# An audio tower on one core: streams laid out time by time, layer 4 in three blocks, and each quad of samples turned alone

## What is computed

```python
h = x[:, None, :]                                    # (64, 1, 4000)
for w, g, b, s in zip(conv_ws, ln_gs, ln_bs, strides):   # 7 convolutions over time, 128 channels
    h = conv1d(h, w, s)                              # taps 10,3,3,3,3,2,2; strides 5,2,2,2,2,2,2
    h = gelu(layernorm_over_channels(h) * g + b)
h = layernorm(h, fln_g, fln_b) @ proj_w + proj_b     # (64, 12, 192)
h = h + attention(layernorm(h))                      # 6 heads over the 12 tokens of a clip
h = h + ffn(layernorm(h))                            # 9 experts: expert 0 for all, the best one for each token
```

## Time and profile before

| | |
|---|---|
| median of 3 runs | 563.9 us (563.47 to 564.89) |
| the profiled execution's own time | 564.41 us |
| its span | 562.6 us |
| TensorE matmul busy | 537.1 us, 95% |
| ScalarE, VectorE, GpSimd busy | 322.7, 309.5, 258.6 us |
| mean granted TensorE clock | 0.98 |

### The profile page before, as it was taken

One profiled execution on the slowest core, in us unless ns is written; L12 is line 12 of the kernel. 1 busy time (PEld: TensorE's weight loads), 2 busy tenths in 40 slices (PEclk: granted clock), 3 DMA queues, 4 the chain that ended last, 5 costly groups with the idle time before them and its releaser, 6 DMA issues.

```text
span 562.6 us, 11208 instructions
## 1 busy us (share of the span) xinstructions
PE 537.1 (95%) x4099; PEld 504.7 (90%) x4099; DVE 309.5 (55%) x767; ACT 322.7 (57%) x557; POOL 258.6 (46%) x298
## 2 busy tenths in 40 slices
PE   6898999999999999999999999999999997899995
PEld 6797989999999999999999999999899886799995
DVE  4665465457567666757575766654564443612231
ACT  1567657747675776677575757773663423444440
POOL 5683464785239427732863394243242120033343
PEclk9999999999999999999999999999999996799998
DMA  7490001692000100000000000000000087151110
GB/s 196 124 276 10 1 15 35 171 239 59 20 1 20 24 5 7 20 22 5 2 20 20 7 20 1 20 6 2 2 6 6 0 218 193 40 142 44 45 39 12
DMA packets 19505, 29.46 MB, mean 52 GB/s; under 512 B 2620, under 2 KB 13846, under 8 KB 19452
## 3 DMA queue, kind: packets, MB, share of 16 engines
q1 hardware_dynamic: 16140, 18.95, 12.7%
q0 software_dynamic: 3296, 9.78, 6.9%
q10 hardware_dynamic: 16, 0.00, 0.0%
HBM read 17.09 MB, written 9.18 MB: 47 GB/s over the span
## 4 chain that ended last, share of the span: by engine, by line
PE 88%; ACT 3%; POOL 2%; DVE 2%; issue 2%; DMA 0%; SPq 0%; POOLq 0%; DVEq 0%; ACTq 0%
PE ps L805 23%; PE ps L797 11%; PE ps L794 8%; PE ps L824 7%; PE ps L1076 5%; PE ps L878 4%; PE ps L1065 3%; PE ps L1064 3%; PE ps L899 3%; PE ps L799 2%; PE ps L795 2%; PE ps L944 2%; PE ps L967 2%; PE ps L887 2%; PE ps L888 1%
## 5 line engine op out<-in xcount | busy, mean ns | idle before, releaser
L649 POOL TENSOR_TENSOR rstd<-ssum,neghalf 128x4 f32<-128x4 f32 (+8 forms) x128 | 116.3, 908 | 195.8 <-DVE ssum L1180 195.4
L805 PE MATMUL ps<-wt,wide 128*124 128x128 f32 (+3 forms) x1248 | 149.5, 274 | 2.5 <-ACT wide L1517 2.1
L805 PEld LDWEIGHTS ps<-wt,wide 128*124 128x124 f32 (+3 forms) x1248 | 142.7, 180 | 5.5 <-issue 2.8
L1486 ACT ACTIVATE work<-ps 128x512 f32<-128x512 f32 (+8 forms) x128 | 66.3, 518 | 131.9 <-PE ps L805 73.0
L1189 DVE TENSOR_TENSOR work<-ps,rstd 128x512 f32<-128x512 f32 (+8 forms) x128 | 75.3, 588 | 75.4 <-POOL rstd L649 71.6
L1180 DVE TENSOR_REDUCE ssum<-work 128x4 f32<-128x516 f32 (+8 forms) x128 | 74.8, 584 | 57.3 <-ACT work L1486 56.9
L643 POOL TENSOR_TENSOR rstd<-var,half 128x12 f32<-128x12 f32 (+3 forms) x39 | 79.0, 2039 | 7.8 <-DVE var L1117 7.2
L1528 ACT ACTIVATE h<-ps,lncol 128x512 f32<-128x512 f32 (+1 forms) x120 | 79.7, 712 | 1.8 <-PE ps L878 1.8
L1503 ACT ACTIVATE wide<-ps,lncol 128x256 f32<-128x256 f32 (+1 forms) x112 | 74.1, 770 | 2.2 <-PE ps L824 2.1
L797 PE MATMUL ps<-wt,h 128*128 128x256 f32 x288 | 70.1, 380 | 0.0
L824 PE MATMUL ps<-ident,work 128*128 128x128 f32 (+3 forms) x416 | 64.8, 268 | 1.2 <-ACT wide L1503 0.8
(11 more groups left out here) (239 smaller groups left out, 825.5 us busy)
## 6 DMA issues: line engine op xcount, KB each, us to landing
sorted_tokens<-zero POOLq DMA_DIRECT2D x1, 5886.5 KB, 30.4
W2s<-in_L_ffn_W_dram SPq DMA_DIRECT2D x9, 576.0 KB, 8.4
wide<-in_L_ffn_W_dram SPq DMA_DIRECT2D x8, 576.0 KB
cols<-cols SPq DMA_DIRECT2D x24, 128.0 KB, 2.2
cols<-sorted_tokens SPq DMA_DIRECT2D x13, 96.5 KB, 1.9
xnat<-in_x_dram SPq DMA_DIRECT2D x7, 130.0 KB, 2.1
wt<-in_L_ffn_b_dram SPq DMA_DIRECT2D x1, 864.0 KB, 5.0
wide<-in_L_tok_conv_w_dram SPq DMA_DIRECT2D x4, 192.0 KB, 3.1
```

The lines of the kernel that those rows point to most:

```text
L649: gp.tensor_tensor(rstd[0:rows, idx, 0:count], ssum[0:rows, idx, 0:count], neghalf[0:rows, 0:count], ALU.pow).then_inc(rstd_done, 1)
L805: last = nc.tensor.matmul(y[0:rows, j * C:(j + 1) * C], h[l - 1][g % 2][:, at:at + rows], wt[:, TAP0[l] + tap, :], start=(tap == 0), stop= ...
L1486: nc.scalar.activation(sq[0:rows, n % 2, 0:CUTS[l][k], 0:C], ybank(n)[0:rows, 0:w].rearrange("p (j c) -> p j c", c=C), ACT.Square).then_in ...
```

## The change

**Layout.** Rows and streams now lie time by time: time 0 of the eight clips, time 1 of the eight clips, and so on. The rows of a sample tile are 16 segments x 8 clips. An odd or even stream is a run of 8 clips per time. There are no unused rows between clips, so the blocks are of 120, 112, 128, 96 and 96 rows in layers 2 to 6 (124, 116, 100, 100, 104 before), and layer 4 takes three blocks a group where it took four. The cuts of layer 2 are 4, 4, 2, 3 (4, 3, 3, 3 before). The paddings go, and with them most of the memsets that cleared them.

**Quads.** `is_pair`, `halves` and `other_copies` go. `xhl` holds a local step's taps as high, low, high, low (40 columns), so a triple is 120 columns, and `xt` turns 17 triples in every group. VectorE copies a quad once, as 120 rows. `xcol` has two buffers (three before). The 24 DMAs that copied halves and the waits on them go.

**Other.** The first weights `w0t` are built on 120 partitions with a simpler mask; `projg` and `w0per` have tiles of their own. `HEAD`, `BODY`, `LAST`, `DRAIN` and the `RUN_` tables are written anew.

```diff
-ROWS_OF = [P, P, 124, 116, 100, 100, 104]
+ROWS_OF = [P, P, 120, 112, P, 96, 96]
-CUTS = [None, (4, 4, 4, 4, 4, 4, 1), (4, 3, 3, 3), (4, 3), (4,), (2,), (1,)]
+CUTS = [None, (4, 4, 4, 4, 4, 4, 1), (4, 4, 2, 3), (4, 3), (3,), (2,), (1,)]
 BODY = [
     ((1, 0, 0), [('xt', 0, 2)], []),
-    ((1, 0, 1), [], []),
+    ((1, 0, 1), [('l0', 0, 2, 0), ('l0', 0, 2, 2)], []),
     ((4, -2, 0), [('l0', 0, 2, 1)], []),
-    ((2, -1, 1), [('l0', 0, 2, 0)], []),
-    ((2, -1, 0), [('l0', 0, 2, 2)], []),
-    ((2, -1, 2), [('l0', 0, 3, 0), ('raw', 1)], []),
-    ((5, -2, 0), [('l0', 0, 3, 2), ('l0', 0, 3, 1)], []),
+    ((2, -1, 2), [], []),
+    ((2, -1, 1), [('raw', 1), ('xt', 0, 3)], []),
+    ((2, -1, 0), [('l0', 0, 3, 1)], []),
+    ((5, -2, 0), [('l0', 0, 3, 0), ('l0', 0, 3, 2)], []),
...
-    ((1, 0, 3), [('xt', 1, 0)], []),
-    ((3, -1, 0), [], [('xs', 1, 1)]),
-    ((3, -1, 1), [('l0', 1, 0, 1), ('l0', 1, 0, 0)], []),
-    ((1, 0, 5), [('l0', 1, 0, 2), ('l0', 1, 1, 1)], []),
-    ((1, 0, 6), [('l0', 1, 1, 0), ('l0', 1, 1, 2)], []),
+    ((1, 0, 3), [('l0', 0, 4, 2), ('xt', 1, 0)], [('pow', 1, 3), ('pow', 1, 4)]),
+    ((3, -1, 0), [('l0', 1, 0, 1), ('l0', 1, 0, 0)], [('pow', 1, 2)]),
+    ((1, 0, 5), [('l0', 1, 0, 2), ('xt', 1, 1)], []),
+    ((3, -1, 1), [('l0', 1, 1, 1), ('l0', 1, 1, 2)], [('xs', 1, 1)]),
+    ((1, 0, 6), [('l0', 1, 1, 0)], []),
 ]
...
 (scale, on VectorE)
-                parts = halves(g, lo, hi)
-                for src, dst in parts:
-                    last = nc.vector.tensor_copy(dst[:, :, :, 0:ROW].bitcast(F32R), src)
-                last.then_inc(s_high, 1)
+                twice = xsc[:, lo:hi, :].unsqueeze(2).to_broadcast([P, n, 2, K0])
+                nc.vector.tensor_copy(xhl5[:, lo:hi, :, 0, :].bitcast(F32R), twice).then_inc(s_high, 1)
                 ve.wait_ge(s_high, k)
-                for src, dst in parts:
-                    last = nc.vector.tensor_tensor(dst[:, :, :, ROW:2 * ROW].bitcast(F32R), src, dst[:, :, :, 0:ROW], ALU.subtract)
-                last.then_inc(s_parts, 1)
+                nc.vector.tensor_tensor(xhl5[:, lo:hi, :, 1, :].bitcast(F32R), twice, xhl5[:, lo:hi, :, 0, :],
+                                        ALU.subtract).then_inc(s_parts, 1)
...
 (job_xt, on VectorE)
-                if is_pair(g, q):
-                    nc.vector.tensor_copy(xcol[m % XC][0:64, 0:w], src[0:64, 0:w]).then_inc(s_upper, 1)
-                    nc.vector.tensor_copy(xcol[last % XC][64:P, 0:w], src[64:P, 0:w]).then_inc(j_dve, 1)
+                nc.vector.tensor_copy(xcol[(QUADS * g + q) % 2][0:12 * K0, 0:w], src[0:12 * K0, 0:w]).then_inc(j_dve, 1)
...
 (SyncE)
-                sp.wait_ge(s_upper, 2 * (g - PAIRED_FROM) + q // 2 + 1)
-                sp.dma_start(up[64:P, :], up[0:64, :]).then_inc(s_dup[m % XC], 16)
-                sp.wait_ge(j_dve, DVE_TO[JOB[("xt", g, q)] + 1])
-                sp.dma_start(low[0:64, :], low[64:P, :]).then_inc(s_dup[(m + 1) % XC], 16)
...
 (turn of layer 1, on TensorE: where a block's rows go in PSUM)
-                        to = bass.AP(at.tensor, at.offset, [at.ap[0], [1, P // 2], [P if d else 3 * P, 2]])
+                        to = bass.AP(at.tensor, at.offset, [at.ap[0], [2 * BT, SEG // 2], [P if d else 3 * P, 2], [1, BT]])
...
 (gelu of layer 1, on ScalarE)
-                        to = bass.AP(at.tensor, at.offset, [at.ap[0], [shift, v.stop - v.start], [1, w], [LEN1, P // 2]])
+                        to = bass.AP(at.tensor, at.offset, [at.ap[0], [BT * shift, v.stop - v.start], [BT * LEN1, SEG // 2], [1, w * BT]])
...
 (gelu of layer 6)
-                    dst = h6[:, :].rearrange("p (b t) -> p b t", b=BT)
+                    dst = h6[:, :].rearrange("p (b t) -> p t b", b=BT)
...
-RUN_7 = {'turn_h': 3, 'stat_h': 2, 'power_h': 2, 'project': 3, ...
+RUN_7 = {'turn_h': 2, 'stat_h': 2, 'power_h': 2, 'project': 4, ...
 (DRAIN, behind the chunk (6, 7, 0))
     (None, [('down', 3)], []),
+    (None, [('up', 2, 1)], []),
+    (None, [('up', 2, 0)], []),
+    (None, [('up', 2, 3), ('up', 2, 2)], []),
+    (None, [('down', 4)], []),
     (None, [], []),
-    (None, [('up', 2, 1), ('up', 2, 0)], []),
-    (None, [('up', 2, 2), ('down', 4), ('up', 2, 3)], []),
     (None, [], []),
     (None, [('up', 2, 5)], []),
```

More of the change, by code:

```diff
@@ L74, in needed @@
     ends = [ROWS_OF[layer - 1] * sum(CUTS[layer - 1][:i + 1]) for i in range(len(CUTS[layer - 1]))]
-    return next((i for i, e in enumerate(ends) if e > 2 * rows), len(ends) - 1)
+    return next((i for i, e in enumerate(ends) if e >= 2 * rows + BT), len(ends) - 1)
 def first_block(layer, k):
@@ L266 @@
             assert ORDER.index((1, was_[0], reads_)) <= min(slot_of(("l0", g_, q_, j)) for j in range(3))
-        if g_ >= 1 and q_ < 2:
-            part_ = next(k for k, row in enumerate(SLOTS) if ("xs", g_, q_) in row[2])
-            assert slot_of(("xt", g_ - 1, (1 if g_ < PAIRED_FROM else 0, 2 if g_ == PAIRED_FROM else 4)[q_])) <= part_
-STEPS = [[] for _ in SLOTS]
-RUN_0 = {'turn_h': 3, 'stat_h': 3, 'power_h': 4, 'project': 5, 'stat_1': 5, 'power_1': 4, 'norm_1': 6, 'turn_1': 8, 'copy_1': 7, 'qkv': 9, 'split_queries': 9, 'split_keys': 9, 'scores': 10, 'mask': 10, 'less_max': 10, 'exp': 10, 'sum_probs': 10, 'turn_probs': 11, 'copy_probs': 11, 'values': 12, 'divide': 12, 'turn_heads': 14, 'copy_heads': 14, 'out_project': 15, 'residual': 15, 'power_2': 15, 'norm_2': 16, 'turn_2': 17, 'copy_2': 17, 'logits': 18, 'choose': 18, 'rank': 21, 'slot': 21, 'scatter': 27, 'fold_weights': 0, 'fold': 1, 'fold_keep': 2}
@@ L275 @@
-RUN_1 = {'turn_h': 3, 'stat_h': 3, 'power_h': 4, 'project': 5, 'stat_1': 5, 'power_1': 4, 'norm_1': 6, 'turn_1': 8, 'copy_1': 7, 'qkv': 9, 'split_queries': 9, 'split_keys': 9, 'scores': 10, 'mask': 10, 'less_max': 10, 'exp': 10, 'sum_probs': 10, 'turn_probs': 11, 'copy_probs': 11, 'values': 12, 'divide': 12, 'turn_heads': 14, 'copy_heads': 14, 'out_project': 15, 'residual': 15, 'power_2': 15, 'norm_2': 16, 'turn_2': 17, 'copy_2': 17, 'logits': 18, 'choose': 18, 'rank': 21, 'slot': 21, 'scatter': 27}
@@ L276 @@
-RUN_5 = {'turn_h': 3, 'stat_h': 3, 'power_h': 2, 'project': 4, 'stat_1': 3, 'power_1': 3, 'norm_1': 5, 'turn_1': 6, 'copy_1': 6, 'qkv': 7, 'split_queries': 7, 'split_keys': 7, 'scores': 8, 'mask': 8, 'less_max': 8, 'exp': 9, 'sum_probs': 9, 'turn_probs': 10, 'copy_probs': 10, 'values': 11, 'divide': 11, 'turn_heads': 12, 'copy_heads': 12, 'out_project': 13, 'residual': 13, 'power_2': 13, 'norm_2': 13, 'turn_2': 14, 'copy_2': 14, 'logits': 15, 'choose': 15, 'rank': 16, 'slot': 16, 'scatter': 19}
@@ L277 @@
[L277 to L278 removed]
+        if QUADS * g_ + q_ >= 2:
+            assert job_at(*divmod(QUADS * g_ + q_ - 2, QUADS)) < JOB[("xt", g_, q_)]
@@ new lines @@
+        if g_ >= 1:
+            part_ = next(k for k, row in enumerate(SLOTS) if ("xs", g_, scaled_for(g_, q_) - 1) in row[2])
+            assert slot_of(("xt", g_ - 1, q_)) <= part_
+STEPS = [[] for _ in SLOTS]
+RUN_0 = {'turn_h': 4, 'stat_h': 4, 'power_h': 4, 'project': 4, 'stat_1': 6, 'power_1': 5, 'norm_1': 6, 'turn_1': 8, 'copy_1': 8, 'qkv': 9, 'split_queries': 9, 'split_keys': 9, 'scores': 10, 'mask': 10, 'less_max': 10, 'exp': 10, 'sum_probs': 11, 'turn_probs': 11, 'copy_probs': 13, 'values': 14, 'divide': 14, 'turn_heads': 15, 'copy_heads': 15, 'out_project': 16, 'residual': 16, 'power_2': 16, 'norm_2': 17, 'turn_2': 18, 'copy_2': 18, 'logits': 19, 'choose': 19, 'rank': 21, 'slot': 22, 'scatter': 25, 'fold_weights': 0, 'fold': 1, 'fold_keep': 2}
@@ new lines @@
+RUN_1 = {'turn_h': 4, 'stat_h': 4, 'power_h': 4, 'project': 4, 'stat_1': 6, 'power_1': 5, 'norm_1': 6, 'turn_1': 8, 'copy_1': 8, 'qkv': 9, 'split_queries': 9, 'split_keys': 9, 'scores': 10, 'mask': 10, 'less_max': 10, 'exp': 10, 'sum_probs': 11, 'turn_probs': 11, 'copy_probs': 13, 'values': 14, 'divide': 14, 'turn_heads': 15, 'copy_heads': 15, 'out_project': 16, 'residual': 16, 'power_2': 16, 'norm_2': 17, 'turn_2': 18, 'copy_2': 18, 'logits': 19, 'choose': 19, 'rank': 21, 'slot': 22, 'scatter': 25}
@@ new lines @@
+RUN_5 = {'turn_h': 3, 'stat_h': 3, 'power_h': 2, 'project': 4, 'stat_1': 3, 'power_1': 3, 'norm_1': 4, 'turn_1': 5, 'copy_1': 5, 'qkv': 7, 'split_queries': 7, 'split_keys': 7, 'scores': 8, 'mask': 8, 'less_max': 8, 'exp': 9, 'sum_probs': 10, 'turn_probs': 10, 'copy_probs': 10, 'values': 11, 'divide': 11, 'turn_heads': 12, 'copy_heads': 12, 'out_project': 13, 'residual': 13, 'power_2': 13, 'norm_2': 13, 'turn_2': 14, 'copy_2': 14, 'logits': 15, 'choose': 15, 'rank': 17, 'slot': 17, 'scatter': 18}
@@ new lines @@
```

(2 more changed lines are left out.)

224 lines of the change are left out of this document (77 added, 147 removed), and 48 rows, old and new, of tables (BODY, HEAD, LAST).

## The result

The changed kernel takes 560.38 us, the median of 10 runs (558.55 to 563.29), against 564.14 us (563.21 to 565.01) of the kernel before in the same job: a ratio of 0.9939, 95% interval 0.9917 to 0.9962. On another chip it was 558.80 against 562.98: 0.9927 (0.9908 to 0.9947). So the change makes the kernel 3.8 to 4.2 us faster by the medians (3.4 to 4.1 by the ratios, which compare means); 2.7 were forecast. Its profiled execution took 559.19 us with a span of 557.5 (before 564.41 and 562.6, so 5.2 less).

The account below looks back on a forecast made before the run. TensorE, 95% busy and never idle in the bodies, was taken as the bound. TensorE's work -0.6, GELU -1.6 and last chain -0.5 gave -2.7 us on 564.4: 561.7, stated as 561.5; own range 559.5 to 562.5, 8-in-10 range 558 to 567.

Parts of the forecast that it names:

- parts 1 and 2: TensorE's work: layer 4's block -5.3 us, narrower turns -0.6, 48 more sample turns +5.3; sum -0.6, a body +0.14.
- rival of a slow round trip: Each singly turned quad's copy through VectorE comes back late, 0.2 us at 30 trips: +6 us, 567.5; chance 0.17.
- The draw: Rival: GELU's gain stays hidden and something else holds the last chain, only -0.6 us: 563.3; chance 0.27.
- part 4: ScalarE: near writes bring layer 1's GELU from 820 to 564 ns, 25 us less ScalarE, -1.6 us on the path.
- The 0.1 us of the prediction: Layer 6's GELU, now writing 48 bytes apart, pays about 0.1 us; one is on the last chain.
- part 5: PSUM: layer 1's turns writing runs of 8 instead of scattered values gain nothing by the rows, though the skill page says cheaper.
- Part 3: VectorE: quad copies cost the same, the sample split 1.1 us more a group but covered; removing 24 DMAs gains nothing.
- At the start ...: nothing: At the start, the removed memsets and single copy of first taps lie beside samples' DMA and GpSimd's power: no gain.
- the conv of group 1 about a microsecond earlier: Sign in the head that would show the forecast right: that convolution starts about a microsecond earlier.
- part 6: Order: bodies keep their cover; in the last chain, moving `turn_h` and one `up` gives about -0.5 us together.
- the narrower turns: TensorE's other turns lose 96 columns a group: 0.08 us a group, 0.6 us in all.

Follow-up runs that it names:

- e7: Changed kernel's layout, three-block layer 4 and order, with the shared turns, half copies and DMAs of the kernel before: 556.44 us, ratio 0.9879 to the kernel before.
- e10: Changed kernel with layer 1's GELU writing values 100 bytes apart as before: 561.20 us, ratio 0.9953 to the kernel before.
- e3: Kernel before with only layer 1's GELU reading and writing in the new pattern, runs of 16: 563.41 us, ratio 0.9993.
- e1: Kernel before with the new layout, GELU and block sizes, but its own order and shared turns: 561.67 us, ratio 0.9977.
- e4: Changed kernel with layer 4 back in four blocks, of 96 rows: 563.77 us, ratio 1.0021 to the kernel before.
- e9: Changed kernel with the old slots from the last group's layer 2 on and old token tables of groups 5 to 7: 559.83 us, 0.9939 of the kernel before.
- e11: The changed kernel itself run once more on another chip, nothing changed: 558.80 us against 562.98 of the kernel before, ratio 0.9927.
- e12: Changed kernel with samples loaded clip by clip as before, second run: 558.77 us beside the changed kernel's 558.80, ratio 0.9896 to 0.9933 (interval).
- e2: Kernel before with every quad turned by itself, in the old layout and order: 575.62 us, ratio 1.0225.
- e8: Changed kernel's layout and order with the old shared turns, plus the first group's products ahead of the first taps' turns: 556.63 us, 0.9877 of the kernel before.

## Why the prediction was right, and where not

**TensorE's work, parts 1 and 2: right for the bodies.** A draw was forecast, +0.14 us a body, and +0.07 was measured. Layer 4's block costs 0.59 us a body (0.66 forecast; the run of 18 takes 2.03 us and not the 1.97 of the count, and the turns are alike, 0.32 us for three of 128 and 0.33 for four of 96) and 4.6 us to the last convolution (5.3). The single turns cost 5.5 us in the kernel before when they are placed well (5.3). The rival of a slow round trip is out for the changed kernel: no idle time of TensorE in its bodies is ended by a copy or by anything else. The draw (563.3) is out as well, for the interval of the ratio ends at 562.0 us.

**But the single turns are not 5.3 us in the new order.** Against e7 they cost 3.1 us in the trace and 0.65 a body, where 0.88 was counted. e7's body (51.20) is 0.16 above the count of work (51.78 - 0.66 - 0.08 = 51.04), the changed kernel's 0.07 below its own. Of the 3.1 us, 2.6 are lost in the four whole bodies and only 0.3 in the head and 0.2 behind the bodies. So the new order suits the single turns, or e7's order suits the pairs less; the runs don't tell which.

**The GELU, part 4: right.** 565 ns against 564 forecast. ScalarE's busy time fell by 17.1 us, not by the 25 of the step: the two GELUs of a pair overlap (a pair took 1.42 us, not 2 x 0.82, and takes 1.03 now), so the group of 96 gave 19.0, and other rows rose by 2. On the path 1.6 were forecast and 1.4 measured in the trace (e10), 1.0 in the old order (e3); no timing shows it clear of noise. No body is touched by it. In the narrow place of the head 0.6 us came (e10) where 0.9 were forecast. By the Trainium skill (SBUF — State Buffer, the section on the DMA port swizzle) each access that crosses to a new line of 16 bytes pays, so layer 6's GELU with its new step of 48 bytes was to be dearer. It went from 427 to 513 ns; the trace agrees. The 0.1 us of the prediction fits this case's price of 1 ns a far value (256 ns more for 256 values).

**PSUM, part 5: right.** Four turns of layer 1, with values 8 in a row, took 0.44 us to the next start after (219.40 to 219.84), and with single values far apart 0.43 before. The same page of the Trainium skill says that non-contiguous PSUM access slows matmuls significantly; these rows give that no support.

**Part 3: the split was mis-sized, without effect.** A group's casts and subtractions cost 0.7 us more by the rows (411 + 658 + 717 + 722 ns against 2 x (286 + 408) + 187 + 214), where 1.1 was forecast. It is hidden as forecast, since no idle time of the bodies ends with it.

**The start: a cost left out.** "At the start ...: nothing" was written of memsets and a copy. The reordered load of the samples, which is part of the layout, was not priced: its issue is 0.27 us longer, and the first convolution 0.55 later. The first convolution starts at 20.09 to 20.59 us in the seven traces with the new loads (the changed kernel, e1, e4, e7, e9, e10, e11), and at 19.55 to 19.80 in those with the old loads whose clock stays up (before, e2, e3). How much of it reaches the end stays open. e8 kept its earlier start up to the last convolution; e12's trace lost it to the clock at once, and the times of its other executions fall on both sides of the changed kernel's. With the later start the sign "the conv of group 1 about a microsecond earlier" failed: it is 0.12 us later (47.85 against 47.73), and 0.43 nearer to the first convolution.

**The last chain, part 6: right by luck.** -0.5 was forecast for `turn_h` and an `up` moved away, -0.66 came. But with the old order the chain takes from 39.39 to 40.82 us and with the new one from 39.89 to 41.41, and much of that is the clock: the same 12 instructions behind the logits take 2.87 us in e1, 3.17 after, and 4.13 both before and in e9. The trace of the kernel before is the longest of its kind. Nothing shows that the moves gave anything.

**The rest: the order in the head, which the forecast had at nothing.** Layer 4 (-4.6), the GELU (-1.4), the single turns (+3.1), the start (+0.55), the drain's order (-0.2 before the last convolution by e9) and the last chain (-0.66, the clock's) make -3.2 of the -5.3 us; the narrower turns, forecast at 0.6, leave 1.5 us. The bodies agree with the count, so most of it lies in the head: from the first convolution to the first whole body it is 119.43 us before and 116.80 after, and e10, e4 and e7 explain only 0.97 + 0.29 - 0.34 = 0.9 of these 2.6 us. e1 and e7 isolate the order there, for they have the same layout and the same shared turns, and differ in slots and token tables alone (first convolutions at 20.36 and 20.59, first whole bodies at):

```profile
139.64 1.46 PE L793 MATMUL ps<-wt,h 128*128 128x256 f32 x6
```

```profile
137.05 1.25 PE L793 MATMUL ps<-wt,h 128*128 128x256 f32 x5
```

The old order takes 119.28 us in the head and the new one 116.46: 2.8 us. e1 is only 0.15 below the kernel before, so part of the 2.8 is what the old order swallowed of the gains of layer 4 and the GELU. Which slot does it stays open. Over the whole kernel the old order gives 561.67 us and the new one 556.44.

So the forecast's total is partly luck. The single turns cost 2.2 us less than counted and the order in the head gave what nobody had counted; layer 4 gave 0.7 less, the start cost 0.55, and the gain of the last chain was not earned. In the same way its sum without the turns, 5.3 + 0.6 + 1.6 + 0.5 = 8.0 us, is near the 7.1 that e7 gained by the medians (8.4 by the profiled executions), but not by these parts alone. The profiled executions of the change differ by 5.2 us and the medians by 3.8: runs of the changed kernel spread by 4.7 us, and those from 563.0 up had a mean clock of 0.975 or 0.976 against 0.984 to 0.988 in those up to 560.0.

## What to carry to other kernels

Where one engine is full, count its instructions by distances between starts: layer 4's block (4.6 us for 5.3) and 48 turns in the old order (5.5 for 5.3) came out within 15% of the count. In the new order the same 48 turns cost 3.1, so a count is no more than a first estimate where the rest of the order can move. But cutting work frees time only if the order covers what the removed work had covered (e1 had 0.74 us less to do in a body and kept none of it, mostly for a GELU behind a table load), and a job added costs its length only where its bank is free (e2 paid 12 us for 5.3). When a change bundles a gain with a price, undo the price alone: the layout and the order are worth 7.1 us by e7, and the single turns give 3 to 4 of them back. And before a difference under 1 us is put down to an edit, look at the same stretch in all traces: the last chain varied by 1.4 us within one order.
